# Three passes instead of full fp32 for one more pair of key blocks in an attention and MoE kernel, with the low parts made on GpSimd and a new order of the work

## What is computed

```python
k = apply_rope(x @ Wk.T)
v = x @ Wv.T
q = apply_rope(jnp.einsum('btd,hkd->bhtk', x, Wq))
scores = jnp.where(causal, jnp.einsum('bhtk,bsk->bhts', q, k) * scale, -jnp.inf)
w = jax.nn.softmax(scores, axis=-1)
out = jnp.einsum('bhts,bsk->bhtk', w, v)      # the "values product"
return out.transpose(0, 2, 1, 3).reshape(B, T, NKV * HS) @ Wo.T
...
h = jax.nn.gelu(jnp.einsum('td,edf->etf', x, W1) + b1[:, None, :])
eo = jnp.einsum('etf,efd->etd', h, W2) + b2[:, None, :]
out = jnp.einsum('te,etd->td', w, eo)
```

## Time and profile before

| | before |
|---|---|
| median of 3 runs | 1719.2 us (1719.08 to 1719.27) |
| the profiled execution: its own time | 1719.58 us |
| its span | 1717.7 us |
| PE busy | 1707.5 us (99%) |
| DVE busy | 1211.3 us (71%) |
| ACT busy | 1012.2 us (59%) |
| POOL busy | 1009.8 us (59%) |

### The profile page before, as it was taken

How to read it: one execution, slowest core, us unless ns; L and a number is a source line. 1 busy time by engine, 2 the same in 40 slices (tenths; PEclk the granted TensorE clock), 3 DMA queues, 4 the chain that set the end, 5 groups by cost and what they waited for, 6 DMA issues and landing times.

```text
span 1717.7 us, 26567 instructions
## 1 busy us (share of the span) xinstructions
PE 1707.5 (99%) x8420; PEld 1440.7 (84%) x8420; DVE 1211.3 (71%) x2282; ACT 1012.2 (59%) x1833; POOL 1009.8 (59%) x1710
## 2 busy tenths in 40 slices
PE   8999999999999999999999999999999999999998
PEld 7889989998888888888888888888888888888887
DVE  7877777777676666666666678766766666666666
ACT  4767777766665555555555566555555555555554
POOL 6744564455446474848383949365856556574842
PEclk9999999999999999999999999999999999999999
DMA  4100000101111111101111101132121011111101
GB/s 117 31 26 20 26 29 19 35 23 54 30 45 39 38 37 38 50 25 49 33 46 33 57 18 51 54 75 87 57 60 49 26 49 38 38 37 37 38 13 50
DMA packets 91835, 72.05 MB, mean 42 GB/s; under 512 B 11824, under 2 KB 89904, under 8 KB 91696
## 3 DMA queue, kind: packets, MB, share of 16 engines
q1 hardware_dynamic: 91552, 70.29, 15.0%
q10 hardware_dynamic: 144, 0.07, 0.0%
HBM read 61.82 MB, written 8.52 MB: 41 GB/s over the span
## 4 chain that ended last, share of the span: by engine, by line
PE 95%; ACT 1%; DVE 1%; issue 1%; POOL 0%; DVEq 0%; ACTq 0%; POOLq 0%
PE bank L1128 13%; PE bank L1126 13%; PE bank L1127 13%; PE bank L1082 12%; PE bank L1084 12%; PE bank L1083 12%; PE bank L1006 3%; PE bank L1032 3%; PE bank L1046 2%; PE bank L996 2%; PE bank L997 2%; PE bank L998 2%; PE bank L1027 1%; PE bank L1028 1%; PE bank L1029 1%; PE bank L921 1%
## 5 line engine op out<-in xcount | busy, mean ns | idle before, releaser
L1415 ACT ACTIVATE g_sb<-c_sb,b_cols 128x512 f32<-128x512 f32 x384 | 276.6, 720 | 393.4 <-DVE c_sb L1928 291.6
L1757 DVE TENSOR_TENSOR h_lo<-g_sb,h_hi 128x512 fp32r<-128x512 f32 x512 | 388.5, 779 | 101.6 <-ACT h_hi L1419 100.8
L1126 PE MATMUL bank<-h_hi,w_both 128*128 128x512 f32 x1024 | 398.8, 389 | 0.0
L1128 PE MATMUL bank<-h_lo,w_both 128*128 128x512 f32 x1024 | 398.7, 389 | 0.0
L1127 PE MATMUL bank<-h_hi,w_both 128*128 128x512 f32 x1024 | 398.4, 389 | 0.0
L2097 POOL TENSOR_TENSOR h2f<-h2f,y_sb 128x256 f32<-128x256 f32 x216 | 200.8, 963 | 293.1 <-DVE y_sb L1781 293.1
L1082 PE MATMUL bank<-t_hi,w_hi 128*128 128x512 f32 x896 | 351.3, 392 | 1.0 <-ACT p_u L1451 0.4
L1084 PE MATMUL bank<-t_hi,w_lo 128*128 128x512 f32 x896 | 348.9, 389 | 0.0
L1083 PE MATMUL bank<-t_lo,w_hi 128*128 128x512 f32 x896 | 348.8, 389 | 0.0
L1419 ACT ACTIVATE h_hi<-c_sb,b_cols 128x512 fp32r<-128x512 f32 x384 | 272.6, 710 | 0.0
L1127 PEld LDWEIGHTS bank<-h_hi,w_both 128*128 128x128 f32 x1024 | 192.2, 188 | 40.1
(11 more groups left out here) (201 smaller groups left out, 2938.1 us busy)
## 6 DMA issues: line engine op xcount, KB each, us to landing
w_raw<-w_dram SPq DMA_DIRECT2D x128, 256.0 KB, 3.1
g_rows<-gates_scratch SPq DMA_DIRECT2D x31, 512.0 KB, 8.3
x_sb<-x_dram SPq DMA_DIRECT2D x32, 128.0 KB, 2.2
x_scratch<-x_sb SPq DMA_DIRECT2D x32, 128.0 KB, 1.7
x_slabs<-x_scratch SPq DMA_DIRECT2D x4, 512.0 KB, 7.6
out_dram<-x_slabs SPq DMA_DIRECT2D x4, 512.0 KB, 3.4
h2f<-x_scratch SPq DMA_DIRECT2D x4, 512.0 KB, 3.8
wmod_raw<-wmod_dram SPq DMA_DIRECT2D x4, 256.0 KB, 3.5
```

Of the source, the lines that this page charges most:

```text
L1126: nc.tensor.matmul(o, w_hi, h_hi[:, ring, :], start=first, stop=False, skip_group_check=True)
L1128: done_ = nc.tensor.matmul(o, w_hi, h_lo[:, ring, :], start=False, stop=last, skip_group_check=True)
L1415: nc.scalar.activation(g_sb[:, m % 2, :], source, ACT.Gelu_apprx_tanh, bias=bias).then_inc(act_g, 1)
L1757: nc.vector.tensor_tensor(h_lo[:, m % RING, :], g_sb[:, m % 2, :], h_hi[:, m % RING, :].bitcast(F32), ALU.subtract).then_inc(dve_lo, 1)
```

## The change

`SPLIT_FROM` goes from 2 to 1: group 1 (key blocks 2 and 3) becomes split too, and with it the values of tiles with `TIME` 2 and 3 (`EARLY` is 2 instead of 4), whose low parts DVE makes. Group 1 is also "relayed" (`RELAYED` is 1): ACT evicts its bank twice, once rounded to `pT_hi` and once as it is into `probs`, whose blocks 2 and 3 have just been read, and POOL, which takes both operands from there, makes `pT_lo`. The maxima `M` of the tile that uses the same `probs` buffer next wait for it. The whole groups keep one slot of `pT` instead of two; the split groups keep three. The planner's table `PATIENCE` is new, so every engine's list is new.

```diff
-SPLIT_FROM = 2
-WHOLE_SLOTS = 2
+SPLIT_FROM, RELAYED = 1, 1
+WHOLE_SLOTS = 1
 SPLIT_SLOTS = 3
 EARLY = 2 * SPLIT_FROM
...
-        return [("POOL", 1500 + 1200 * (i >= 31), [("norm", i, 0, "ACT")])]
+        return [("POOL", (1500 if i >= BEHIND else 950) + 1200 * (i >= 31), [("norm", i, 0, "ACT")])]
...
+            if groups_of(i - PBUF) > RELAYED:
+                after.append(("T", i - PBUF, RELAYED, "POOL"))
...
-        parts = [("PE", 218 * n, [("E", i, 1, "ACT")]), ("ACT", 180 + 212 * n, [("T", i, g, "PE")] + after)]
+        parts = [("PE", 218 * n, [("E", i, 1, "ACT")]),
+                 ("ACT", (180 + 212 * n) * (1 + (g == RELAYED)), [("T", i, g, "PE")] + after)]
+        if g == RELAYED:
+            return parts + [("POOL", 100 + 620 * n, [("T", i, g, "ACT")])]
...
-        "rstd": (2233, 3141, 1932, 2437), "traw": 1292, "split": 3035,
+        "rstd": (1084, 2724, 2277, 2829), "traw": -2119, "split": 2879, "T": (1032, 3, 1396, 927),
...
-                        nc.scalar.activation(to[:, PT_SLOT[stage], 0:n], tr_ps[T_BANK[stage]][:, 0:n],
-                                             ACT.Copy).then_inc(act_T, 1)
+                        made = nc.scalar.activation(to[:, PT_SLOT[stage], 0:n], tr_ps[T_BANK[stage]][:, 0:n], ACT.Copy)
+                        if g == RELAYED:
+                            made = nc.scalar.activation(left_in_probs(i, g), by_blocks(tr_ps[T_BANK[stage]][:, 0:n]), ACT.Copy)
+                        made.then_inc(act_T, 1)
...
                             dve.wait_ge(*done(pe_T, "T", i - PBUF, groups_of(i - PBUF) - 1))
+                            if groups_of(i - PBUF) > RELAYED:
+                                dve.wait_ge(*low_made(("T", i - PBUF, RELAYED)))
...
+                    elif kind == "T":
+
+                        part = slice(0, len(blocks_of(i, g)) * NH * P)
+                        slot = PT_SLOT[stage]
+                        pool.wait_ge(*done(act_T, *stage))
+                        nc.gpsimd.tensor_tensor(by_blocks(pT_lo[:, slot, part]), left_in_probs(i, g),
+                                                by_blocks(pT_hi[:, slot, part].bitcast(F32)),
+                                                ALU.subtract).then_inc(pool_T, 1)
```

More of the change, by code:

```diff
@@ L248, in parts_of @@
         after = [("PV", *before[1:], "PE")] if before else []
-        parts = [("PE", 218 * n, [("E", i, 1, "ACT")]), ("ACT", 180 + 212 * n, [("T", i, g, "PE")] + after)]
+        parts = [("PE", 218 * n, [("E", i, 1, "ACT")]),
+                 ("ACT", (180 + 212 * n) * (1 + (g == RELAYED)), [("T", i, g, "PE")] + after)]
+        if g == RELAYED:
+            return parts + [("POOL", 100 + 620 * n, [("T", i, g, "ACT")])]
         return parts + [("DVE", 150 + 269 * n, [("T", i, g, "ACT")])] if is_split(g) else parts
     if kind == "PV":
-        after = [("T", i, g, "DVE" if is_split(g) else "ACT")]
+        after = [("T", i, g, "POOL" if g == RELAYED else "DVE" if is_split(g) else "ACT")]
         if g == 0:
@@ L270 @@
     "PE": {
-        "aT": (606, 858, 701, 754), "bT": (676, 872, 1068, 936), "qkv": (1036, 1207, 1076, 1039),
-        "rotT": (840, 875, 904, 892), "Y": (591, 802, 835, 970), "pre": 1535, "gate": 1413,
-        "S": (587, 868, 859, 1011), "T": (582, 866, 871, 984), "PV": (926, 923, 916, 1018),
+        "aT": (562, -3316, -2974, 823), "bT": (901, 928, 774, 1234), "qkv": (1466, 1156, 1367, 1327),
+        "rotT": (825, 846, 952, 1201), "Y": (993, 923, 535, 1211), "pre": 1524, "gate": 1963,
+        "S": (785, 1042, 845, 1231), "T": (1136, 964, 867, 1276), "PV": (1303, 1047, 921, 1323),
     },
     "ACT": {
[L276 to L279, removed]
+        "aT": (-385, -27, -213, -7839), "xb": (-5103, -3063, -173, 1272), "bT": (-5916, -407, 857, 99),
+        "qkv": (253, -3734, 431, 701), "rotT": (345, -4827, -3388, -5947), "O": (-5160, -4028, 589, -4137),
+        "norm": (500, 497, -3080, -3625), "pre": 240, "wq": -2087, "G1": 275, "traw": 608, "tsum": 1250,
+        "E": (370, 848, 1224, 722), "T": (-170, 299, 853, -747),
     },
     "DVE": {
[5 rows of a table removed]
[3 rows of a table added]
+        "gate": -2704, "tsum": 864, "tlo": -399, "M": (-1814, -1994, -304, -3652), "N": (-4170, -2516, -1471, -3928),
+        "T": (-1812, -6484, -4046, -13093),
     },
     "POOL": {
-        "xa": (2507, -6705, -479, 2273), "rope": (2382, 1899, 1931, 1975), "norm": (1231, 1179, -1475, 1817),
-        "rstd": (2233, 3141, 1932, 2437), "traw": 1292, "split": 3035,
+        "xa": (2691, 3167, 3331, 2720), "rope": (1424, 2089, 112, 2939), "norm": (1113, 2862, 2208, 1410),
+        "rstd": (1084, 2724, 2277, 2829), "traw": -2119, "split": 2879, "T": (1032, 3, 1396, 927),
     },
@@ L304, in reader_of @@
     if kind == "T":
-        return "DVE" if is_split(stage[2]) else "ACT"
+        return "DVE" if is_split(stage[2]) and stage[2] != RELAYED else "ACT"
     if kind == "qkv":
@@ L564, in adaln_block @@
         pool_cos, pool_sin, pool_even, pool_odd = sem("pool_cos"), sem("pool_sin"), sem("pool_even"), sem("pool_odd")
-        pool_var, pool_ln, pool_xa = sem("pool_var"), sem("pool_ln"), sem("pool_xa")
+        pool_var, pool_ln, pool_xa, pool_T = sem("pool_var"), sem("pool_ln"), sem("pool_xa"), sem("pool_T")
         dve_affine, dve_xa, act_xb, dve_T, dve_V = sem("dve_affine"), sem("dve_xa"), sem("act_xb"), sem("dve_T"), sem("dve_V")
@@ L685, in v_split, with by_blocks, left_in_probs @@
             return dve_V, sum(TIME[n] >= EARLY for n in range(i + 1))
+        def by_blocks(a):
+            return a.rearrange("p (j h c) -> p j h c", h=NH, c=P)
+        def left_in_probs(i, g):
+            turned_keys = slice(2 * g * P, (2 * g + len(blocks_of(i, g))) * P)
+            return probs[i % PBUF][:, :, turned_keys].rearrange("p h (j c) -> p j h c", c=P)
         def low_made(stage):
-            return dve_T, sum(is_split(s[2]) for s in STAGES["T"][0:AT[stage]])
+            if stage[2] == RELAYED:
+                return pool_T, sum(s[2] == RELAYED for s in STAGES["T"][0:AT[stage]])
+            return dve_T, sum(s[2] > RELAYED for s in STAGES["T"][0:AT[stage]])
         bank_a, bank_b, bank_g, bank_h = (bank[:] for bank in banks[0:4])
@@ L906, in wait_t_read @@
                     if was[0] == "T":
-                        pe.wait_ge(*(low_made(was) if is_split(was[2]) else done(act_T, *was)))
+                        pe.wait_ge(*(low_made(was) if was[2] > RELAYED else done(act_T, *was)))
                     elif was[0] == "aT":
```

## The result

The changed kernel takes **1727.0 us** (median of 5 runs, 1725.71 to 1727.22) against 1719.2 (1719.0 to 1719.4) before: ratio 1.0041, 95% interval [1.003, 1.0053]. It is 7.8 us slower, where 2.7 were forecast, and outside the range. The profiled execution has a span of 1725.2 us, 7.5 more than before.

A forecast was written before the change was run, and what follows sets the result against it. PE's work plus its few waits bounds the kernel, with POOL setting the pace at short tiles. −3.9 (work) + 1.0 (start) + 2.4 (tiles 4 to 6) + 3.2 (tiles 17 to 20) = +2.7 us: 1721.9 us, range 1716.2 to 1724.8.

The forecast's parts named there:

- The removed work: On PE, 54 blocks of group 1 take 0.36 instead of 0.432 us each: 3.9 us less work.
- The start: Batch 1's rows' product, 1.72 us, moves behind tile 2's `PV`, where PE has no idle time: net +1.0 us.
- The new operation: POOL's subtraction for group 1's low part, 28 times: 1.29 us each, 0.75 for two of half width.
- The rival of 1.66: POOL's new operation takes 1.66 instead of 1.29 us at some ten tiles: 3.7 us, 1725.6 us; chance 0.14.
- The sentence on the port's rule: DVE instructions with two SBUF inputs block POOL's SBUF reads, single-input ones don't; so the new operation keeps 1.29 us.
- Tiles 4 to 6: Waits of PE behind POOL's `pT_lo` and `rope` at the early short tiles: together +2.4 us.
- the forecast's own three waits: PE waits 1.2 us for tile 6's `rotT`, 0.3 for tile 7's and 0.9 for tile 5's second `PV`.
- ACT is done at 1.6: At tile 4, ACT finishes group 1's two evictions 1.6 us after the end of its transposes.
- Tile 17: Group 1's `PV` comes 2.5 us of work after its transposes, the low part after 3.1: 0.6 us wait.
- Tile 19: POOL's token parts, `norm`, `rope` and `rstd` delay `pT_lo` to 12.3 us against PE's 9.7: wait of 2.6 us.
- the case of tile 19: Sign of error: the prediction is wrong if PE's wait at tile 19 is under 1.5 us.
- That the waits are hidden: Rival: POOL's list runs ahead, only the 3.9 and the start's 1.0 or less remain: 1715.5 to 1716.5 us; chance 0.19.

The follow-up runs named there:

- e15: Changed kernel with e12's lists searched further, no two gate products close together: 1717.81 us, ratio 0.9989.
- e13: Kernel before, without the change, with searched lists that keep the other engines' work for the attention's end as early: 1717.38 us, ratio 0.9989.
- e7: Changed kernel with batch 1's modulation rows back ahead of tile 2's `rotT` on PE and DVE: 1725.73 us, ratio 1.0035.
- e1: Changed kernel with two of three parts of batch 1's `wo` products later in DVE's list, at tiles 8 and 9: 1725.95 us, ratio 1.0033.
- e2: Changed kernel with the three raw token parts later in ACT's and POOL's lists, at tiles 25 to 27: 1733.4 us, ratio 1.0076.
- e9: Changed kernel with tile 21's `rope` ahead of tile 19's `norm` on POOL and the token parts later: 1724.82 us, ratio 1.0031.
- e5: Changed kernel with 3, 8 and 7 pairs of constant-tile matmuls put into PE's three long waits: 1725.46 us, ratio 1.0034.
- e3: Changed kernel with the moves of e1 and e2 together: 1733.71 us, ratio 1.008.
- e6: Changed kernel without the relay: ACT evicts group 1 once, DVE instead of POOL makes its low part: 1728.62 us, ratio 1.0052.
- e10: Changed kernel with all engines' lists searched from those of before, without the rule that protects the end: 1726.0 us, ratio 1.0044.
- e8: Kernel before with the first four DVE operations of batch 1's `wo` moved directly ahead of tile 4's third low part: 1719.84 us, ratio 1.0002.
- e12: Changed kernel with searched lists that keep the other engines' work for the attention's end as early: 1719.05 us, ratio 1.0.
- e14: Kernel before with one gate product moved, so that two stand directly behind each other near 384 us: 1720.84 us, ratio 1.0009.

## Why the prediction was wrong

- **The removed work** was right: 3.9 us, and e15 against e13 shows the same. The 54 whole products are two records each: 108 fewer, against 162 more three-pass ones.
- **The start** was right: +1.1 measured with the waits near 47 and 54, +1.0 forecast, and e7 gives 1.3 back.
- **The new operation** was right: 26 of 128x512 at 1.30 us on POOL against 1.29, two of half width at 0.73. The rival of 1.66 did not come. It stretched where DVE's operation with both inputs in SBUF ran beside it (1.68 at 236.90, with DVE's `t_f` at 236.78). The sentence on the port's rule was used on one side only: the same rule, read from DVE's side, fits what `wo` did. The Trainium skill ("SBUF — State Buffer", Who interferes with whom) says that DVE's instructions with two SBUF inputs contend with GpSimd's reads, and that a plain `tensor_scalar` can too, in a mode that uses both ports. The prediction's sentence, that one with a single SBUF input doesn't, left this case out. The rows agree: 0.84, 0.98 and 1.10 beside POOL, 0.43, 0.30 and 0.42 away from it. The second of the four, at 61.52, kept its 0.29; POOL's `rot_c`, which began just behind it at 61.53, took 1.15 for 1.02.
- **Tiles 4 to 6: the step that failed** is "Count from the end of tile 4's group-1 transposes". The count followed POOL alone, as the part said ahead of it ("What counts is what stands behind these 1.3 us in POOL's list"). The group behind has its low part from DVE, and DVE's list, with four operations of `wo` ahead of it, wasn't counted. The wait was 2.3 there, and the forecast's own three waits (1.2, 0.3, 0.9) hid in it. They are real: e1 shows them as 1.0, 0.3 and 0.8. "ACT is done at 1.6" failed too: ACT had `xb` to do first, was done some 2.6 us behind the transposes, and tile 4's own second product, which the sum put at nothing, waited 0.8. The waits of this part were thus 3.1 instead of 2.4.
- **Tile 17**: 0.15 instead of 0.6. **Tile 19**: the size was right, 2.65 at two places (1.91 and 0.74) for 2.6 at one, the reason was not. The prediction hung it on the token parts ("the token parts can't begin before tile 17's last `PV`"). e2 took them away and the waits stayed. By the rows two things held POOL at the same time, the parts (to 231.66) and a `norm` that DVE made late (231.5), with tile 21's `rope` behind both; e9 moved the `rope` and the parts, and the wait fell to 0.9. That the order of `norm` and `rope` alone would do it is not shown.
- **The step that was missing** is the clock. The working added up waits as if PE went on at full speed behind them. Behind the two long ones the granted clock was 0.50 for a few us each: 2.7 us in all, a third of the slowdown, of which 0.8 would else have been a wait. With PE's idleness filled (e5) it did not fall. With the same two waits at tiles 17 and 19 it fell in the changed kernel, e1, e3 and e7, and not in e2, so a wait of this size makes the fall likely, and not certain.
- Of "wrong if", the case of tile 19 held in the letter: its own product waits 0.7, and the larger wait stood just ahead, at the transposes of tile 17's second norm. The largest new wait, at tile 4, was in none of the places named.
- **The rivals.** That the waits are hidden was wrong for the kernel as it is, and right as a possibility: in e15 they are.

## What to carry to other kernels

Where a new operation is put on an engine with room, look at every engine's list at the places where the order is tight, not only at the one that gets the work: a wait is as long as the latest of them. Price a long wait of PE (here those of about 2 us) at one and a half times its length, since the clock fell behind 12 of the 16 waits of 1.9 us or more that the profiles show; filling it with matmuls that do nothing brings part of that back. When an order is made anew together with a change, give the old kernel a new order as well before judging the change: here the order alone was worth 1.8 us to the kernel before, and the change with its first order cost 7.8.

## What was not expected of the hardware

- The clock fell to 0.50 behind waits of 2.3 us with 0.8 just ahead (64 us), of 1.9 and 0.7 (239 us), 3.2 (e6, at 64 us) and 2.7 (e10, at 398.7). It stayed behind waits of 0.9 (e8, e9) and 1.0 (e1), and also behind those of 2.4 at 392.4 in e10, 2.5 at 296 in e2, 1.9 at 239 in e6, and 1.9 and 0.7 at 237 in e2. So near 2 us the length of a wait alone doesn't decide it.
- A busy PE isn't a working PE: in e12 the clock fell behind 32 matmuls of 36 columns that showed as 4.00 of 4.00 us busy, and in e14's profile it did not. What decides there is open.
- DVE's operations on 128x256 in SBUF take 2 to 3.3 times as long beside POOL's: 0.30 becomes 0.98 and 0.43 becomes 0.84 and 1.10, while POOL's `rope` rows there grow from 1.02 to 1.15 at most. At 236.90 it is POOL's operation that grows, from 1.30 to 1.68, beside a DVE operation that had begun 0.12 earlier.
